# Graph network kernel: second products placed inside the last steps of the first edge stage, and extra TensorE multiplications at the start

## What is computed

```python
# layer 0: message per edge, maximum per destination
feat = concatenate([x[dst], x[src] - x[dst]], axis=-1)
out = segment_max(relu(feat @ W1 + b1) @ W2 + b2, dst)     # 0 where a node has no edge
x = layernorm(x + out)
# layer 1: sum of the neighbours' rows, then a small MLP with a residual product
agg = segment_sum(x[src], dst)
h = maximum((x + agg) @ W1 + b1, 0) @ W2 + b2
x = layernorm(x + (x @ Wres + bres) + h)
```

## Time and profile before

| | |
|---|---|
| median of 3 runs | 1106.35 us (1105.72 to 1106.82) |
| the profiled execution, its own time | 1106.44 us |
| its span, first to last instruction | 1104.6 us |
| PE busy | 1071.8 us (97%) |
| DVE, ACT, POOL busy | 935.3, 898.5, 768.1 us |
| chain that ended last | PE 83%, DVE 6%, ACT 4% |
| mean granted TensorE clock | 0.996 of full |

### The profile page before, as it was taken

The page is one execution under the profiler, slowest core; times in us unless marked ns, Lnnn a source line. Parts: engine busy times, 40 slices in busy tenths (PEclk is TensorE's granted clock), DMA queues, the critical chain, the costliest instruction groups (busy, mean ns, idle before and its releaser), DMA issues.

```text
span 1104.6 us, 27142 instructions
## 1 busy us (share of the span) xinstructions
PE 1071.8 (97%) x7463; PEld 835.7 (76%) x7463; DVE 935.3 (85%) x3649; ACT 898.5 (81%) x3891; POOL 768.1 (70%) x798
## 2 busy tenths in 40 slices
PE   6899999999999999999899999999999999999997
PEld 4677777777666667666578888888888878888886
DVE  7888898887888888888868787878787789999994
ACT  4888888887888888888797888888888887777776
POOL 6777777777777777773047777777777777777722
PEclk9999999999999999999999999999999999999999
DMA  5888778774888888888576666676666566767752
GB/s 160 239 242 239 239 236 240 241 233 136 233 230 229 242 235 222 227 233 222 163 223 198 207 200 203 201 205 202 196 188 172 187 199 215 217 218 219 222 188 96
DMA packets 172255, 231.86 MB, mean 210 GB/s; under 512 B 25658, under 2 KB 90791, under 8 KB 172106
## 3 DMA queue, kind: packets, MB, share of 16 engines
q1 hardware_dynamic: 145434, 180.66, 53.0%
q0 software_dynamic: 25088, 48.94, 17.4%
q10 hardware_dynamic: 1584, 0.53, 0.2%
HBM read 129.48 MB, written 102.78 MB: 210 GB/s over the span
## 4 chain that ended last, share of the span: by engine, by line
PE 83%; DVE 6%; ACT 4%; issue 3%; DMA 0%; SPq 0%; POOL 0%; DVEq 0%; ACTq 0%; POOLq 0%
PE psY L1182 15%; PE psY L1183 15%; PE psH L1194 14%; PE psT L1175 7%; PE psE L1175 5%; PE psE L1324 5%; PE psE L1263 4%; PE psE L1182 4%; PE psE L1183 4%; PE psE L1360 4%; DVE shared L787 3%; ACT junk L993 2%; PE psE L1307 2%; PE psE L1309 2%; PE psE L1315 2%
## 5 line engine op out<-in xcount | busy, mean ns | idle before, releaser
L1182 PE MATMUL psY<-wc,hT 128*128 128x128 f32 x1568 | 304.1, 276 | 2.9 <-ACT o_rows L1018 2.7
L1183 PE MATMUL psY<-wcr,xT 128*128 128x128 f32 x1568 | 303.6, 275 | 0.0
L541 POOL DMA_INDIRECT edge_rows<-x1e_table,idx x196 | 190.2, 970 | 114.2 <-issue 59.4
L545 POOL DMA_INDIRECT out<-edge_rows,idx x196 | 195.1, 995 | 95.1 <-issue 57.9
L1182 PEld LDWEIGHTS psY<-wc,hT 128*128 128x128 f32 x1568 | 240.4, 192 | 16.5 <-issue 13.6
L993 ACT ACTIVATE junk<-psY 128x128 f32<-128x128 f32 x784 | 209.7, 302 | 46.5 <-PE psY L1183 46.4
L1183 PEld LDWEIGHTS psY<-wcr,xT 128*128 128x128 f32 x1568 | 238.6, 192 | 0.0
L541 POOL DMA_INDIRECT edge_rows<-in_x,idx x196 | 190.4, 971 | 64.9 <-issue 59.1
L638 DVE TENSOR_SCALAR x<-x_in,mv,rs 128x128 f32<-128x128 f32 x784 | 220.9, 360 | 0.5
L1194 PE MATMUL psH<-xT,wc 128*128 128x512 f32 x392 | 204.7, 604 | 3.5 <-ACT xT L988 1.7
L993 ACT ACTIVATION_READ_ACCUMULATOR junk<-psY 128x1 f32 x784 | 180.9, 233 | 0.0
(11 more groups left out here) (129 smaller groups left out, 2037.1 us busy)
## 6 DMA issues: line engine op xcount, KB each, us to landing
x_in<-in_x SPq DMA_DIRECT2D x196, 256.0 KB
out<-o_rows SPq DMA_DIRECT2D x195, 256.0 KB
src_bc<-src_dram SPq DMA_DIRECT2D x49, 256.0 KB, 4.6
mask<-mask_dram SPq DMA_DIRECT2D x98, 128.0 KB
x1eT_spill<-x1eT SPq DMA_DIRECT2D x49, 256.0 KB, 2.6
x1e_table<-edge_rows SPq DMA_DIRECT2D x49, 256.0 KB, 3.4
x1e_table<-shared SPq DMA_DIRECT2D x49, 256.0 KB, 4.0
x1eT<-x1eT_spill SPq DMA_DIRECT2D x49, 256.0 KB, 3.0
```

Source lines behind the costliest of these rows:

```text
L541: nc.gpsimd.indirect_dma_start(to, None, table, bass.IndirectOffsetOnAxis(idx[:, what, t:t + 1], 0)).then_inc(landed[n % FLIGHT], 16)
L545: nc.gpsimd.indirect_dma_start(table, bass.IndirectOffsetOnAxis(idx[:, SCAT, t:t + 1], 0), frm, None, bounds_check=limit, oob_is_err=False ...
L1182: t_.matmul(to[:, cut(t)], h[:, cut(t)], wc2[:, :], start=t == 0, stop=False, skip_group_check=True)
L1183: last = t_.matmul(to[:, cut(t)], xt[:, cut(t)], wcr[:, :], start=False, stop=t == TILES - 1, skip_group_check=True)
```

## The change

TensorE's queue alone is changed; every other engine's instructions stay in their order, since the calls that are moved from `walk` into `step_a` stand at the same place there.

```diff
             for s in range(GROUPS, STEPS):
-                step_a(s, None, 0)
-                dense(A_LAST + s - GROUPS)
+                step_a(s, A_LAST + s - GROUPS, A_STEPS)
...
                         first_product(n - 1)
-                    if h >= 2:
+                    if h == A_STEPS:
+                        second_product(n - 2)
+                    elif h >= 2:
                         second_half(n - 2, h - 2)
                 transpose_x1e(s - 2)
                 center_z(s - 1)
                 transpose_in(s + 1)
+                if h == A_STEPS:
+                    first_half(n)
...
+            def spend(n):
+
+                for _ in range(n):
+                    t_.matmul(psE[3][:, 0:P], center[:, :], center[:, :], start=True, stop=True)
+
             pe.wait_ge(s_c, 1)
+            spend(8)
             pe.wait_ge(s_dv, 1)
             for h in range(2):
                 last = t_.transpose(psE[0][:, cut(h)], idx_f[:, 0, h, :], ident[:, :])
             last.then_inc(s_pe, 1)
             transposed(0)
+            spend(4)
             pe.wait_ge(s_w, 16 * 6)
             pe.wait_ge(s_dv, SRC_IDX_STEP + 1)
             t_.matmul(psE[2][:, 0:P], center[:, :], raw[:, W1R, :], start=True, stop=True)
             t_.matmul(psE[2][:, P:2 * P], wtmp[:, 0, :], center[:, :], start=True, stop=True)
             t_.transpose(psE[2][:, 2 * P:3 * P], raw[:, W2R, :], ident[:, :]).then_inc(s_pe, 1)
+            spend(2)
             walk(head, dense, lead_s, step_s, lead_a, step_a, lead_b, step_b)
```

More of the change, by code:

```diff
@@ L452, in step_a @@
                 load_mask(s + 1)
+                if h == A_STEPS:
+                    dense(n)
             def feed_b(g):
@@ L808, in step_a @@
                 copy_xs(s + 1)
-                if n is not None:
+                if h == A_STEPS:
+                    dense(n)
+                elif n is not None:
                     if h == 0:
```

## The result

| | before | changed |
|---|---|---|
| median, us | 1105.86 (6 runs, 1105.09 to 1106.82) | 1110.76 (6 runs, 1109.60 to 1112.32) |
| ratio | | 1.0047, 95% interval 1.0037 to 1.0057 |
| profiled execution, its own time | 1106.44 | 1112.32 |

The change makes the kernel 4.9 us slower, twice the 2.4 us that were forecast. That is 0.5%, and the 95% interval does not take in 1. Its six runs form two groups: three from 1109.60 to 1109.82 with a mean granted clock of 0.996 to 0.997, and three from 1111.70 to 1112.32 with 0.993 to 0.994. The profile is of the second group.

The account below looks back on a forecast made before the run. TensorE bounds the full stretches, a ring through ACT and DVE the border between edge stages. 1106.44 + 2.1 (waits) + 1.5 (clock) - 1.1 (start) = 1108.9, less 0.09 over the median: 1108.8 us; range 1106.6 to 1110.8.

Parts of the forecast that it names:

- The border's waits: Between the edge stages, at full clock: TensorE waits for ACT's finishes and enters the full stretch at 570.44, +2.1 us.
- The last leg: End of the border: from ACT's finish of unit 71 to TensorE's entry into the full stretch, 3.49 us as before.
- The clock at the border: The half clock leaves 550 and falls at 555 to 557 behind the new idle gap, +1.5 us.
- a half-speed stretch of about 3.4 us: Over unit 71's second product and the transposes behind it, ACT waiting; costs nothing to at most 1.7 us, taken as +1.5.
- Rival (b): At the border the clock falls at both new gaps or stays low for two stretches: 1.7 more, 1110.5; chance 0.12.
- The start: Added products raise TensorE's clock early, so DVE gets the last weights (L902) sooner: -1.1 us, from -1.34 to +0.4.
- all of it is passed on unless a load comes late: L902's gain at the start, up to 1.34 us, reaches TensorE's first full stretch behind its DVE wait at 42.44.
- rival (c): The start brings nothing, as the clock rises too late or an `x_in` load is next late: 1110.1; chance 0.06.
- The sign of being wrong that was named: At the start: L902 on DVE moves earlier but TensorE's 42 us point does not.
- Rival (d): At the border unit 71's second product does not wait long and TensorE's own queue decides: -3.9, 1102.5; chance 0.08.
- Rival (a): At the border the clock holds through the new gap: 2.1 - 1.1, 1107.4; chance 0.28.
- The page's rule on transposes: Transposes do not count as busy for the clock, so the border gap starts at 552.1; fall surer, price unchanged.

Follow-up runs that it names:

- the one move: Kernel before with only the second product of unit 70 moved, those of units 71 and 72 left in place, no added products: 1105.31 us, ratio 0.9990.
- the changed kernel again: The changed kernel itself, unaltered, timed once more beside the kernel before: 1109.35 us, ratio 1.0037.
- the moves alone: The changed kernel without the 14 added products at the start, only the moved second products: 1111.64 us, ratio 1.0046 to the kernel before.
- the added products alone: Kernel before with only the 14 added products at the start, queue at the border as before: 1104.53 us, ratio 0.9987.
- the first wait filled: Changed kernel with 15 centring-matrix products ahead of unit 71's second product, the wait ahead of unit 72's left empty: 1109.24 us, ratio 1.0029 to before.
- The early load: Kernel before with the 14 added products, and SP issuing unit 4's load right behind unit 3's: 1104.08 us, ratio 0.9979.
- the filled kernel of before: Kernel before with 8 centring-matrix products in TensorE's first wait of step 49, no second product moved: 1104.59 us, ratio 0.9986.

## Where the prediction held and where it failed

- **The border's waits: right.** +2.1 us was worked out with the clock at full; the two profiles of the changed order without a fall have +2.2. The idle stretch ahead of unit 71's product was forecast as 3.7 us and is 3.67 and 3.68; its start as 556.3, and is 556.16. The mechanism (finish of unit 69, then x1e's transposes behind the product) is the one that the profile shows, and the experiment with the one move takes it away. The last leg was luck. The sum took the 3.49 us from ACT's finish of unit 71 to the entry over from before, where TensorE waited for that finish. In the changed order TensorE's last wait is one product earlier, for the copy of xT (567.54 in the changed kernel again). Unit 75 follows 3.31 us later, TensorE's own pace for a unit; that the finish (567.38) also stands 3.47 us ahead of it is chance.
- **The clock at the border: direction right, mis-sized.** The step that failed is "a half-speed stretch of about 3.4 us", with "at most 1.7". It was sized by the one fall of before, whose stretch was over after 3.4 us. The profile has 6.8 us and then 3.4, together +3.98. Two things were overlooked. The stretch can be twice as long: in the four cases where the clock fell 0.7 to 1.1 us ahead of the work (the first falls here and with the moves alone, the added products alone, the first wait filled; all read in stretches of 0.2 us) it lasted 6.8 us, in the five where it fell 0.3 to 0.55 us ahead or inside the work 3.4. No experiment set that moment, so this is only what the rows have in common. And a second fall came, behind an idle stretch of 2.14 us and 0.6 us of work at full clock. Rival (b) named two falls or two stretches, and had both; at 0.12 it was too small, if the lower mean clock is its sign: 7 of 17 runs of this order have 0.993 to 0.994 (3 of 6, 2 of 5, 2 of 6), and the two of them with a trace show both falls. Its 1.7 us were too little too. Of the other ten, one has a trace, without any fall. Two figures of the passage are off without a part in the sum: from 546.63 to the fall at 550.0 it is 3.4 us and not 3.6, and from 548.3 on TensorE works some 2.8 us of the 8, since the 2.3 leave out the four transposes.
- **The start: mechanism right, mis-sized.** The term was -1.1 and measured -0.27 in the profiled pair, -0.46 between the means of eleven profiles. TensorE's part came out as worked out (13.46 for a forecast of 13.3 to 13.8, clock up before 8.3). The step that failed is "all of it is passed on unless a load comes late": the load of unit 4 was the next thing late, by 0.97 us. I had the condition, as rival (c), and gave it a chance of 0.06 without asking when that load is issued. It stands in SP's queue behind eight more index loads than that of unit 3, and goes out at 13.49. The early load gives the -1.39 back. The sign of being wrong that was named (L902 moves and the 42 us point does not) came all but fully.
- **The sum.** 2.1 + 1.5 - 1.1 = 2.5 was forecast; 2.2 + 3.95 - 0.27 = 5.9 is in the profiled pair, 4.9 between the medians. The two failed terms err on the same side. The range held the time by 0.04 us (1110.76 for 1110.8), and that is luck: the median lies in the gap between the two groups, and the whole slower group is outside.
- **Rival (d)**, a gain by TensorE's own queue: refuted twice, by the 3.68 us idle stretch and by the filled kernel of before. Rival (a), the clock holds: seen in one profile (the changed kernel again, 1108.89), at +2.2 in the middle.
- **The page's rule on transposes** (the same page of the Trainium skill, Part 4: PE-mode transpose) was to make the fall surer. It did not fall in one profile of the same stretch, and no run here tells transposes from products by themselves.

## What to carry to other kernels

A wait is filled at no cost only with work that is ready at that moment and on which nothing queued behind it depends. The product of unit 70 met this; the 0.9 us that it gained are the clock that it kept up, and useless products in its place gain no less. Those of 71 and 72 needed an ACT result 3.7 and 2.8 us away and held up the very engine that makes it. Where an engine idles and others set the pace, useless products that keep TensorE's clock up were worth as much as moved work here, and delayed nobody, since they ended ahead of the release.

Before a gain at the start is counted, ask of each load behind it when it is issued, not only whether it was waited for: a load that just comes in time is the next bound.

## What the runs showed of the hardware that was not expected

- The same program and the same idle stretch of TensorE (3.67 and 3.68 us) ended with the granted clock at 1.00 in one execution and at 0.50 for 6.8 us in another. A price for the clock has to be given as two cases.
- A fall came after an idle stretch of 2.80 us too, and one 0.6 us into the work behind an idle stretch of 2.14 us.
- Every half-clock stretch at the border lasted 3.4 or 6.8 us: 6.8 in the four cases where the clock fell 0.7 to 1.1 us ahead of the work, 3.4 in the other five.
- What a half clock costs depends on who waits: 3.98 us for 10.2 us of it in the changed order. In the order of before 3.4 us of it cost 0.80 to 0.96 us, and 6.8 us (the profile of the added products alone, from 548.8 to 555.6) 0.41 more than that.
- The issue of one edge store on SP took 0.43 us in twelve profiles and 1.30 and 1.39 in two, at the same place of the program; the load behind it moved with it. The long form comes with a packet of the queue q8, kind instruction, beside the issue, as do 107 of 117 issues of more than 1.1 us in six traces.
